# A third buffer for the fc weights of the feed-forward layer, loaded two steps ahead

## What is computed

```python
def _bitlinear(x, w_latent):
    scale = clip(mean(abs(w_latent), axis=1, keepdims=True), 1e-05, None)
    tern = clip(round(w_latent / scale), -1.0, 1.0)
    return x @ (tern * scale).T            # value of the expression in the forward pass

def _L0_ffn_ref(x, fast_b, w_fc, w_proj, u, v, gate):   # w_fc [4096, 1024], w_proj [1024, 4096]
    h = _bitlinear(x, w_fc) + gate * (x @ v.T @ fast_b.T @ u.T)   # rank 16
    r = maximum(h, 0.0)
    return _bitlinear(r * r, w_proj)

x = x + _L0_attn_a_ref(_layernorm(x), ...)   # sl1: 64 heads, window of 128
x = x + _L0_ffn_ref(_layernorm(x), ...)      # sl2
x = x + _L0_attn_b_ref(_layernorm(x), ...)   # sl3: causal, 16 heads
x = x + _L0_ffn_ref(_layernorm(x), ...)      # sl2 again
x = x + _L1_attn_a_ref(...)                  # sl5: linear attention
x = x + _L1_ffn_ref(...)                     # sl6: attention over 16 gated projections
x = x + _L1_attn_b_ref(...)                  # sl7: causal, one head of 1024
x = x + _L1_ffn_ref(...)                     # sl6 again
```

## Time and profile before

| | us |
|---|---|
| median of 2 runs | 12016.07 |
| lowest, highest | 12009.78, 12022.37 |
| the profiled execution | 11997.61 |
| its span, first to last instruction, slowest core (0) | 11995.7 |
| shortest span of a core (2) | 11918.4 |
| TensorE busy, core 0 | 6455.5 (54%) |
| VectorE busy, core 0 | 4617.1 (38%) |
| ScalarE busy, core 0 | 1970.1 (16%) |

### The profile page before, as it was taken

The page is one execution under the profiler, slowest core; times in us unless marked ns, Lnnn a source line. Parts: engine busy times, 40 slices in busy tenths (PEclk is TensorE's granted clock), DMA queues, the critical chain, the costliest instruction groups (busy, mean ns, idle before and its releaser), DMA issues.

```text
span 11995.7 us, 117436 instructions; the slowest of 8 cores (11918.4 to 11995.7 us)
## 1 busy us (share of the span) xinstructions
PE 6455.5 (54%) x39696; PEld 3361.8 (28%) x40058; DVE 4617.1 (38%) x12484; ACT 1970.1 (16%) x6360; POOL 15.9 (0%) x30
## 2 busy tenths in 40 slices
PE   1766666650016666556565665643664556556544
PEld 0332332320002223333332221323552012245510
DVE  1555464633331112444443112354334751333366
ACT  1223232321121111112232101111001010100000
POOL 0000000000000000000000000000000000000000
PEclk9777777775558987555555997775996557678755
DMA  6011101011213331000000334004331110013201
GB/s 100 16 32 27 39 20 40 19 45 53 61 45 73 83 83 37 8 8 1 8 1 12 82 83 84 18 11 57 75 76 28 34 50 21 7 41 74 56 25 59
DMA packets 1063918, 507.73 MB, mean 42 GB/s; under 512 B 893020, under 2 KB 1042945, under 8 KB 1060516
## 3 DMA queue, kind: packets, MB, share of 16 engines
q1 hardware_dynamic: 1052820, 441.15, 13.9%
q0 software_dynamic: 10512, 59.05, 3.9%
HBM read 533.96 MB, written 83.89 MB: 52 GB/s over the span
## 4 chain that ended last, share of the span: by engine, by line
PE 32%; DMA 31%; DVE 21%; ACT 8%; issue 5%; another core or an unknown queue 2%; SPq 2%; DVEq 0%; ACTq 0%; POOL 0%; POOLq 0%
DMA abf<-s2fcT 6%; DMA abf<-s6o 5%; DMA abf<-s2prT 5%; ACT abf L861 4%; DVE X L1296 3%; DMA abf<-s6v 3%; DMA abf<-s6k 3%; DMA abf<-s6q 3%; DVE stat L1683 3%; PE pb L821 3%; DVE stat L938 2%; PE pbig L1656 2%; PE pbig L912 2%; PE pbig L914 2%; PE pb L1711 2%
## 5 line engine op out<-in xcount | busy, mean ns | idle before, releaser
L1177 PE MATMUL pb<-abf,xn_fm 128*128 128x128 bf16 x12288 | 862.5, 236 | 514.4 <-DMA abf<-s6q 171.7
L1177 PEld LDWEIGHTS pb<-abf,xn_fm 128*128 128x128 bf16 x12288 | 802.1, 107 | 574.7 <-issue 574.7
L1296 DVE SCALAR_TENSOR_TENSOR X<-pbig,af,X 128x512 f32<-128x512 f32 x1024 | 721.5, 746 | 275.5 <-DMA abf<-s6o 192.2
L1280 PE MATMUL pbig<-abf 128*128 128x512 bf16 x1002 | 509.4, 609 | 484.7 <-DMA abf<-s6o 357.0
L226 PE MATMUL pt<-ident_bf,abf 128*128 128x128 bf16 x1112 | 141.0, 301 | 1031.7 <-DVE abf L506 819.3
L1199 DVE SCALAR_TENSOR_TENSOR abf<-pb,af,abf 128x128 f32<-128x128 f32 x1440 | 405.6, 344 | 752.5 <-DMA abf<-s6v 217.7
L674 PE MATMUL pbig<-abf 128*128 128x512 bf16 x2008 | 522.5, 403 | 283.5 <-DMA abf<-s2prT 272.1
L645 PE MATMUL pb<-xn_fm,abf 128*128 128x512 bf16 x2000 | 517.1, 401 | 246.0 <-DMA abf<-s2fcT 228.4
L861 ACT ACTIVATE abf<-pbig,stat 128x256 bf16<-128x256 f32 x1024 | 468.3, 482 | 575.3 <-PE pb L821 575.0
L912 PE MATMUL pbig<-mask_w,ident_bf 128*128 128x256 bf16 x960 | 332.2, 346 | 312.4 <-ACT abf L861 302.5
L851 DVE TENSOR_SCALAR abf<-pb,af 64x512 bf16<-64x512 f32 x512 | 384.0, 750 | 244.8 <-PE pb L821 239.2
(11 more groups left out here) (308 smaller groups left out, 9167.0 us busy)
## 6 DMA issues: line engine op xcount, KB each, us to landing
abf<-s2fcT SPq DMA_DIRECT2D x256, 256.0 KB, 2.9
abf<-s2prT SPq DMA_DIRECT2D x512, 128.0 KB, 2.2
abf<-s1q SPq DMA_DIRECT2D x128, 256.0 KB, 2.9
abf<-s1o SPq DMA_DIRECT2D x256, 128.0 KB, 2.2
abf<-s6q SPq DMA_DIRECT2D x128, 256.0 KB, 2.8
abf<-s6k SPq DMA_DIRECT2D x128, 256.0 KB, 2.8
abf<-s6v SPq DMA_DIRECT2D x128, 256.0 KB, 2.8
abf<-s6o SPq DMA_DIRECT2D x256, 128.0 KB, 2.1
```

The costliest lines, as they stand in the source:

```text
L1177: inst = e.matmul(self.pb[pbk][:, tl * 128:(tl + 1) * 128], self.xn_chunk(ic)[:, t * 128:(t + 1) * 128], wbuf[w][:, ic, :], start=(ic == 0 ...
L1280: inst = e.matmul(self.pb[b0 + i], ao_fm[:, t, :], wobuf[e_ % 2], start=True, stop=True)
L1296: t=t: e.scalar_tensor_tensor(xs, self.pb[b0 + i], rw[:, t, em:em + 1], xs, ALU.mult, ALU.add))
```

## The change

In the W1 loop the two buffers of 8 x 128 columns become three. Load w goes to buffer and semaphore oc % 3. Ahead of each quarter's loop loads 0 and 1 are issued in one phase, and in the phase of step oc load oc+2 is issued in place of load oc+1. The matmuls, the number of loads and what each phase needs (load oc for step oc) stay the same. The arena's later tiles move up by 1024 columns.

```diff
         r2 = self.abf.take3(32, 512)
-        w1buf = [self.abf.take3(8, 128), self.abf.take3(8, 128)]
+        w1buf = [self.abf.take3(8, 128) for _ in range(3)]
         w2buf = [self.abf.take(512) for _ in range(4)]
...
         def issue_w1(oc):
-            w = oc % 2
+            w = oc % 3
             return P.dma("sync", f"dW1{w}", lambda e, oc=oc, w=w: e.dma_start(
...
         for quar in range(4):
-            w1tgt = {0: issue_w1(0)}
+            w1tgt = {0: issue_w1(0), 1: issue_w1(1)}
             P.phase()
             for oc in range(34):
                 if oc < 32:
                     pbk = 4 + (oc % 2)
-                    P.need(f"dW1{oc % 2}", w1tgt[oc])
+                    P.need(f"dW1{oc % 3}", w1tgt[oc])
                     def mkh(e, oc=oc, quar=quar, pbk=pbk):
                         for ic in range(FC):
-                            e.matmul(self.pb[pbk], w1buf[oc % 2][:, ic, :],
+                            e.matmul(self.pb[pbk], w1buf[oc % 3][:, ic, :],
...
                     P.op("tensor", mkh)
-                    if oc + 1 < 32:
-                        w1tgt[oc + 1] = issue_w1(oc + 1)
+                    if oc + 2 < 32:
+                        w1tgt[oc + 2] = issue_w1(oc + 2)
```

## The result

The changed kernel takes 11867.2 us in the median (11847.2 to 11901.8, 7 runs) against 12017.4 us before (12002.3 to 12037.2, 6 runs). The ratio is 0.9877, 95% interval 0.986 to 0.9894: 148 us less, 1.2%. Forecast were 11884 us and 1.1%.

The account below looks back on a forecast made before the run. The prediction took the W1 loop to be bound by one weight load in flight at a time; -135.7 (waits) + 3 (starts) - 5 (clock gain) + 6 (limited clock) = -132 us, giving 11884 us, range 11850 to 11985.

Parts of the forecast that it names:

- What bounded the loop: W1 loop: SP waits for each load before issuing the next, so a step is landing plus 0.07 us.
- The waits, -135.7 + 3: W1 loop: hiding loads saves 135.7 us of TensorE idle time in 225 steps; two loads at each start cost 3.
- The floor of 0.26 us: Handshake between two W1 steps (semaphore up, wait passed, weights loaded), claimed to hold in either version.
- The start of a stretch: W1 stretches: two loads issued at once share the DMA engines, costing 0 to 5 us over eight stretches, taken as +3.
- The clock's gain, -5: W1 loop: without idle time from late loads TensorE's clock should not fall, saving 5 us (0 to 15).
- The limited clock, +6: W1 loop: more steps at a lowered clock, each giving back 0.41 us, a stretch 12.3; half a stretch expected, +6.
- The sum: Core 0: -135.7 + 3 - 5 + 6 = -132 us, against the median 11884 us, 1.1% less.
- Which core ends last: Whole program: core 3 gains about 110 us and ends at about 11860, no later than core 0 at 11864.
- C: Rival, W1 loads: they overlap badly and the step becomes their service time; 60 us slower or up to 12316; chance 0.06.
- D: Rival, W1 steps: something else all steps pass keeps them near 2.9 us, time stays at 12016; chance 0.07.
- What would show it: Signs in the profile after: VectorE's load waits nearly none, W1 steps 2.47 us apart, stretches about 715 us together.

Follow-up runs that it names:

- the slower layout: Fc weights stored in DRAM as 2 KB pieces 8 KB apart: on the kernel before, ratio 1.0053; on the changed kernel, ratio 0.9856.

## Why the prediction was right, point by point

**What bounded the loop.** The mechanism was right. One load in flight, the step its landing plus queue work. Shown by the third buffer alone (no change), by SP freed of its wait (a third of the gain) and by the slower layout, which costs 64 us with one load in flight and nothing with two.

**The waits, -135.7 + 3.** Idle time ahead of L645 on core 0 fell by 131.9 us, against 132.7. The floor of 0.26 us held in all 248 steps: 65.8 / 248 = 0.265. The start of a stretch cost what was allowed: the six first waits went from 34.2 to 36.4 us.

**The clock's gain, -5.** Too small: TensorE's busy time on core 0 fell by 15.2 us. Summed step by step from the trace, 7.2 us of it were matmul time above 2.21 us in the middle of stretches; after the change there is none, on any core (before, 3 to 24 us; of the 22 and 24 of cores 2 and 3 about half is the limited clock). Loads of over 4 us still come (5.1 at most on core 3), but TensorE doesn't stop for them and its clock doesn't fall. Another 3.7 us were nine steps at the limited clock, at the head of the fifth stretch, that core 0 had before and not after. The remaining 4 us were at the starts of stretches, where some steps run at the 1.2 GHz level in both kernels: 32.7 us above 2.21 before and 28.7 after on core 0, but 27.3 and 29.5 in the mean over the cores. So about half of this term is the mechanism named. The rest is scatter of the limited clock and of the starts, and that it came out as a gain on core 0 is luck.

**The limited clock, +6.** It was 0 on core 0 in the profile after, and 3.7 us in that before. Its price per step (0.41 us) was right where it occurred, and per stretch (12.3) about right: 11.2 on core 7 and 10 to 15 on core 3. Expecting more of it because the loop is denser was the weak point; the twelve profiles show no such tie. The Trainium skill's rule ("TensorE: Matmul & The Clock Gate", "Seeing it yourself") of a whole die held at 13/16 while several cores run dense matmuls fits the level seen here (granted clock 0.81, 2.26 us for 1.89) but not the reach: in the W1 stretches one pair of cores had it at a time, and most W1 stretches of all eight cores ran without it.

**The sum.** -131.9 - 15.2 = -147.1 us on core 0 (stretches: -147.6), for -132. The 15 us between them are the clock: its gain was 10 us larger than the 5 allowed, most of that by scatter, and the 6 set against it did not come. Both terms are small beside the waits, so the forecast of 11884 for 11867 rests on its mechanism.

**Which core ends last.** I had cores 0 and 3 end together near 11860 us. Core 3 ended last, at 11855.0, 114.5 us less than before for about 110 forecast. Core 0 ended at 11811.7, 52 us below its forecast: 16 us of that in the W1 stretches, 36 outside them. The prediction took the rest of the program as fixed. On core 0 the limited clock held for 517 us in all before and 220 after, which fits, but isn't shown to be the reason.

**The rivals.** C (loads that don't overlap well): the median landing rose from 2.9 to 3.0 us, far from the 4 that would have meant C. Its prices were worked out from a step of 2.93 us, which is short: the mean of the 225 steps was 2.21 + 194.2 / 225 = 3.07. D (something else at the same length): the steps are 2.46. **What would show it** named VectorE's waits (from 225 to 2 on core 3), eight first steps of TensorE at about 43 us (36.4 + 9.2 = 45.6), stretches of 89 us (87.2 in the mean on core 0), a DMA share up to 0.41 (it is 0.41 to 0.44) and W2 loops of unchanged length (between the W1 stretches of core 0 they took 604.3 us before and 606.7 after).

## What to carry to other kernels

Where a step's first wait ends with a load, and the load's landing and the step have the same length, the loads are serial: look at what the issuing queue waits for before the next one, and give it a lead of two steps. The price is one buffer, the gain is the wait above the handshake floor, and it can be read off one view (waits in us and times) before anything is built; for four more loops here that gave 693 us for 650 expected, on top of the changed kernel. Ask as well which engine bounds the step once the load is hidden: in `sl6`'s output projection it is VectorE. In the W1 loop a lead of two steps made greater depth, the slower layout and the late loads stop mattering.

## What was not expected of the hardware

- The landing of a 256 KB load depends on where its pieces lie and hardly on their size: 1024 pieces of 256 bytes 2.9 us, 128 pieces of 2 KB at a pitch of 8 KB 3.1 us, the same without gaps 2.6 us (medians, core 0). Small pieces without gaps were not tried.
- A late load can cost twice: TensorE waits, and then its clock is lower for the next one to three steps. On core 0 the second price came to 7.2 us of the 148 gained.
- The late loads are not random. In the kernel before, 130 of the 2048 loads on all cores took over 3.7 us, 124 of them loads 2, 6, 10, 14, 22 and 26 of a stretch. In 120 of the 130 a transfer of 16 KB on the queue that the profile names "instruction" began while the load was under way. The 144 loads with such a transfer landed after 3.98 us in the median, the others after 2.88. In the changed kernel the late ones are the loads issued in the same steps, which are now one load further on, and beside them load 1, which is issued right behind load 0. So the late loads seem to go with the fetching of the program itself; no run varied that. The DMA view of core 0 over the load of 4.27 us in the earlier trace rows (queue: packets, MB, share) shows one such transfer, and that over the load of 2.82 us before it shows none:

```profile
q1 hardware_dynamic: 1040, 0.26, 27.8%
q8 instruction: 1, 0.02, 2.3%
```

- The third clock level (granted clock 0.81, eight matmuls in 2.26 us in place of 1.89) comes on pairs of cores, mostly for about 160 us at a time by the granted clock in the traces, and not at the same places in two executions of one kernel.
